# The one-hots of a node within its block of 128 go from VectorE to GpSimd in the counting stage of a four-layer graph network

## The reference, cut to what matters

```python
summed = segment_sum(x[src], dst)            # layer 0: mean over the edges of a node
cnt    = segment_sum(ones, dst)
h      = (summed / max(cnt, 1)) @ W_l + b_l + x @ W_r       # then batch norm, relu
...
out_deg = segment_sum(ones, src)             # layer 1: normalised convolution
h       = x * rsqrt(max(out_deg, 1))
agg     = segment_sum(h[src], dst) * rsqrt(max(in_deg, 1))  # then @ W + b
...
# layer 2: attention over the edges with a tensor product; layer 3: relu messages over the edges
```

## Time and profile before

| | |
|---|---|
| median of 3 runs | 6073.1 us (6062.63 to 6097.11) |
| profiled execution, own time | 6084.07 us |
| its span, first to last instruction | 6082.3 us |
| counting stage, first to last one-hot | 103.8 to 702.1 us |
| VectorE busy in 300 to 500 us | 198.05 of 200 us |
| ScalarE busy in 300 to 500 us | 150.89 of 200 us |
| GpSimd busy in 104 to 705 us | none |

### The profile page before, as it was taken

The page is one execution under the profiler, slowest core; times in us unless marked ns, Lnnn a source line. Parts: engine busy times, 40 slices in busy tenths (PEclk is TensorE's granted clock), DMA queues, the critical chain, the costliest instruction groups (busy, mean ns, idle before and its releaser), DMA issues. The chain is left out here.

```text
span 6082.3 us, 95707 instructions
## 1 busy us (share of the span) xinstructions
PE 4642.1 (76%) x21193; PEld 3132.0 (51%) x21193; DVE 4743.6 (78%) x9453; ACT 2345.0 (39%) x4962; POOL 3215.8 (53%) x4106
## 2 busy tenths in 40 slices
PE   2887567588888888888888888888885555555566
PEld 1322223366666666666666666666662554554454
DVE  6999853499999999999999999999995443433344
ACT  1777500155555555445555555455541000000001
POOL 0000000167766776667667777676662565555563
PEclk7999879599999999999999999999995555555555
DMA  2111134366666666666666666666641333333332
GB/s 60 74 74 84 63 149 165 84 146 141 144 141 142 147 143 138 139 140 143 142 144 145 141 140 140 139 146 140 138 103 38 82 80 77 79 78 79 77 82 48
DMA packets 540385, 692.83 MB, mean 114 GB/s; under 512 B 191096, under 2 KB 302648, under 8 KB 536248
## 3 DMA queue, kind: packets, MB, share of 16 engines
q1 hardware_dynamic: 485752, 608.80, 40.9%
q0 software_dynamic: 52288, 81.11, 6.0%
q10 hardware_dynamic: 2240, 1.78, 0.1%
HBM read 636.60 MB, written 54.79 MB: 114 GB/s over the span
## 5 line engine op out<-in xcount | busy, mean ns | idle before, releaser
L1539 POOL DMA_INDIRECT msg_rows<-a_rows,msg_idx x808 | 795.1, 984 | 571.3 <-ACT msg_idx L1511 295.1
L1114 POOL DMA_INDIRECT attn_rows<-x_twice,attn_idx x808 | 899.5, 1113 | 223.6 <-issue 214.4
L1063 ACT CAST attn_z_hi<-attn_z 128x512 fp32r<-128x512 f32 x1010 | 622.4, 620 | 666.0 <-DVE attn_z L1346 373.5
L1352 DVE TENSOR_TENSOR attn_z_lo<-attn_z,attn_z_hi 128x512 fp32r<-128x512 f32 x808 | 823.4, 1019 | 18.7 <-ACT attn_z_hi L1063 1.3
L1577 PE MATMUL msg_at_dst<-msg_bwin,msg_pick 128*128 128x64 f32 x1616 | 397.7, 428 | 573.6 <-DVE msg_pick L1603 337.5
L1151 POOL TENSOR_TENSOR attn_vx<-attn_ex,attn_vw 128x512 f32<-128x512 f32 x202 | 327.4, 1621 | 791.8 <-ACT attn_ex L1090 791.8
L1346 DVE TENSOR_TENSOR attn_z<-attn_xt,attn_sh 128x512 f32<-128x512 f32 x1010 | 684.1, 694 | 21.4 <-ACT attn_xt L1046 1.2
L1577 PEld LDWEIGHTS msg_at_dst<-msg_bwin,msg_pick 128*128 128x128 f32 x1616 | 360.0, 328 | 649.0 <-DVE msg_pick L1603 370.5
L843 POOL TENSOR_TENSOR x_t<-x_t,ln_rec 64x416 f32<-64x416 f32 x12 | 12.7, 1058 | 1147.7 <-DVE ln_rec L832 1147.7
L1630 DVE TENSOR_TENSOR acc<-acc,msg_sums 64x128 f32 x808 | 225.8, 279 | 463.1 <-remote 282.4
L1517 ACT ACTIVATE msg_msg<-msg_pre 128x256 f32<-128x256 f32 x202 | 84.2, 417 | 1238.3 <-DVE msg_pre L1618 679.2
(11 more groups left out here) (265 smaller groups left out, 11957.9 us busy)
## 6 DMA issues: line engine op xcount, KB each, us to landing
attn_sh<-in_edge_sh SPq DMA_DIRECT2D x404, 640.0 KB
attn_dst<-dst_scaled SPq DMA_DIRECT2D x202, 256.5 KB
attn_feat<-in_edge_feat SPq DMA_DIRECT2D x404, 128.0 KB
attn_qwin<-q_rows SPq DMA_DIRECT2D x808, 64.0 KB
msg_dst<-dst_scaled SPq DMA_DIRECT2D x202, 256.0 KB
counts<-chunk SPq DMA_DIRECT2D x15, 3100.0 KB, 9.7
chunk_late<-counts SPq DMA_DIRECT2D x15, 3100.0 KB, 10.4
msg_bwin<-b_rows SPq DMA_DIRECT2D x808, 32.0 KB
```

The source lines that it names most:

```text
L1063: nc.scalar.copy(z_hi[p][:, c, :], z[:, c % 2, :]).then_inc(high_sb, 1)
L1114: pool.indirect_dma_start(rows[p][:, t, :], None, dram["x_twice"], bass.IndirectOffsetOnAxis(ap=idx[p][:, t:t + 1], axis=0)).then_inc(rows ...
L1352: dve.tensor_tensor(z_lo[p][:, c, :], z[:, c % 2, :], z_hi[p][:, c, :].bitcast(F32), ALU.subtract).then_inc(low_ready, 1)
L1539: pool.indirect_dma_start(rows[p][:, t, :], None, dram["a_rows"], bass.IndirectOffsetOnAxis(ap=idx[p][:, t:t + 1], axis=0)).then_inc(rows_ ...
```

## The change

GpSimd gets a program of its own in the counting stage. It makes `lo_hot`, three `tensor_scalar` per group, behind the same wait for the ring as VectorE has. VectorE keeps `key_hot`, behind its own copy of that wait, and the additions. The semaphore `hot` becomes two, `key_made` and `lo_made`, and TensorE waits for both.

```diff
@@ VectorE
                 for s in range(SLOTS):
-                    nc.vector.tensor_scalar(lo_hot[g % RING][:, s, :], sb["lo_iota"][:], sb["lo_tab"][:, s, g:g + 1],
-                                            None, ALU.is_equal)
                     ts = nc.vector.tensor_scalar(key_hot[g % RING][:, s, :], sb["key_iota"][:],
                                                  sb["key_tab"][:, s, g:g + 1], None, ALU.is_equal)
-                ts.then_inc(hot, 1)
+                ts.then_inc(key_made, 1)
@@ GpSimd
+        @block.gpsimd
+        def _(pool):
+            for g in range(NG):
+                if g >= RING:
+                    pool.wait_ge(counted, g - RING + 1)
+                for s in range(SLOTS):
+                    ts = nc.gpsimd.tensor_scalar(lo_hot[g % RING][:, s, :], sb["lo_iota"][:],
+                                                 sb["lo_tab"][:, s, g:g + 1], None, ALU.is_equal)
+                ts.then_inc(lo_made, 1)
@@ TensorE
-                pe.wait_ge(hot, g + 1)
+                pe.wait_ge(key_made, g + 1)
+                pe.wait_ge(lo_made, g + 1)
```

More of the change, by code:

```diff
@@ L449, in count_and_sum @@
         ph = Phase(nc, ctx, "count")
-        piece_step, pieces_done, cleared, hot, counted, evacuated, applied, added, tallied, reduced = (
-            ph.sem(n) for n in ("piece_step", "pieces_done", "cleared", "hot", "counted", "evacuated",
+        piece_step, pieces_done, cleared, key_made, lo_made, counted, evacuated, applied, added, tallied, reduced = (
+            ph.sem(n) for n in ("piece_step", "pieces_done", "cleared", "key_made", "lo_made", "counted", "evacuated",
                                 "applied", "added", "tallied", "reduced"))
```

## The result

| | before | after |
|---|---|---|
| median | 6080.66 us (6062.63 to 6097.11, 4 runs) | 6412.02 us (6402.59 to 6426.31, 4 runs) |
| profiled execution, own time | 6084.07 us | 6426.31 us |
| first to last 128-column one-hot | 103.8 to 701.9 us, VectorE | 88.9 to 972.5 us, GpSimd |
| first to last row-wise maximum of the attention loop | 1211.4 to 4552.7 us | 1481.8 to 4871.9 us |

The change makes the kernel slower: the ratio is 1.0537, with a 95% interval of 1.0509 to 1.0565, 331 us by the medians. The forecast was 6221 us, 140 us above the median before, and its range ended at 6390 us. The sign was right, but by another mechanism than the forecast's, so it is no merit of the sum; the size was not right.

What follows compares the result with a forecast made beforehand. VectorE was taken to bound the counting stage; 0.805 us work plus 0.80 us stall made 1.605 us a group against 1.287, +148 us over 465 groups. Forecast 6221 us; whole range 6020 to 6390.

Steps and rivals of the forecast that it cites:

- the sum: Counting stage: 0.80 us stall on 0.805 us VectorE work, 1.605 us per group against 1.287, times 465: +148 us.
- What bounds the kernel: Counting stage, 598.3 us: VectorE is full and sets the pace at 1.287 us per group until another engine takes over.
- The pace of the next engine: Counting stage: with VectorE relieved, TensorE and ScalarE would set about 1.05 us per group, a gain of 109 us.
- What VectorE gives up: Counting stage: three 128-column one-hots at 0.16 us each leave VectorE, whose work falls from 1.285 to 0.805 us per group.
- What GpSimd takes on: Counting stage: a GpSimd one-hot costs 0.30 us, between 0.20 and 0.41; three make 0.90 us per group, below 1.05.
- GpSimd is itself the bound: Rival, counting stage: the GpSimd instruction costs 0.55 us, a group 1.97 us, +315 us, 6388 us; chance 0.16.
- What the two engines do to each other: Counting stage: VectorE stands still during GpSimd's burst of three one-hots, 0.80 us of stall per group; chance 0.60.
- the eight in a row: Attention loop row cited as evidence: a VectorE subtraction lasted 3.96 us instead of 0.69, waiting for eight successive GpSimd additions.
- the full stall: Counting stage: VectorE waits for all three GpSimd one-hots of a group, less about 0.10 us for the first one's start.
- The ring, the additions, the stages up to the attention loop: GpSimd runs ahead by the ring's four groups, so its waits cost nothing; additions and neighbouring stages do not change.
- Nothing after 760 us changes: Everything after the counting stage, the attention loop included, was claimed to keep its time: 0 us.
- TensorE's clock: Rival, counting stage: the granted clock falls, some 30 us more; expected to hold with TensorE 64% busy; no separate chance.

Runs made afterwards that it cites:

- e6: Changed kernel, but GpSimd makes its 128-column one-hots for the first four groups only, later groups reuse them: 6012.57 us, ratio 0.9902 to the kernel before.
- e1: Changed kernel, but GpSimd makes only one of the three 128-column one-hots per group, VectorE the other two: 5995.02 us against 6077.91 before, ratio 0.9867.
- e11: Changed kernel, but GpSimd makes one 128-column one-hot in even groups and two in odd ones, VectorE the rest: 6101.61 us, ratio 1.003 to the kernel before.
- e5: Changed kernel, but VectorE makes its 400-column one-hots for the first four groups only, later groups reuse them: 6345.23 us in one run.
- e3: Changed kernel, but GpSimd makes only the first 64 of the 128 columns of each one-hot: 6163.96 us in one run.
- e2: Changed kernel, but GpSimd makes two of the three 128-column one-hots per group, VectorE the third: 6108.78 us, ratio 1.0053 to the kernel before.
- e13: Kernel before plus 1395 one-column memsets on GpSimd in the counting stage that nothing waits for: 5860.52 us, one run, on a chip where the kernel before takes 5786.
- e15: Kernel before plus 465 one-column memsets on GpSimd in the counting stage that nothing waits for, on another chip: 5760.45 us against 5785.75, ratio 0.9954.
- e12: Kernel before plus 12 one-column memsets on GpSimd in the counting stage that nothing waits for, on another chip: 5859.12 us against 5785.68, one run.
- e8: Changed kernel, but GpSimd takes the minimum of the row and the number per partition in place of the comparison: 6388.93 us, one run.
- e4: Changed kernel, but GpSimd compares a row of fp32 numbers in place of fp16 ones: 6398.98 us, one run.
- e7: Changed kernel, but GpSimd compares with the constant 5 in place of the number per partition from the table: 6389.36 us, one run.

## Why the prediction was wrong, point by point

- **What bounds the kernel:** right. VectorE set the pace, and with its 128-column one-hots gone (e6) the stage is 146 us shorter. The pace of the next engine was mis-sized: 0.964 us, not 1.05.
- **What VectorE gives up:** right by direction; e1 and e11 came out at 1.165 and 1.170 us a group, from sums of the distances of the earlier trace rows that give 1.125 and 1.045 and some hold-up.
- **What GpSimd takes on:** this step failed, and it is the main one. I took 0.30 us with bounds of 0.20 and 0.41, from an affine select and an iota and a two-input addition. Measured: 0.585 us nearly alone (e5), 0.634 in the stage. The upper bound was no bound: a two-input row doesn't cover another instruction with one input. The case was there as the rival *GpSimd is itself the bound*, at 0.55 us and +315 us, with a chance of 0.16; it is what happened, and the stage itself gave +271. It put the instruction too cheap (0.55 for 0.585 us) and the hold-up too dear (0.315 for 0.15 us a group); that its 1.97 us is so near to the 1.90 measured is in part luck. The Trainium skill (GPSIMD Engine Reference, sections 3.1 and 4.1) puts one-input work at about line rate, 1.03 cycles per element; the 2.66 ns a column of e3 are three times that at 1.2 GHz, so the measurement decides against it for this instruction.
- **What the two engines do to each other:** this step failed too, the other way. I took the eight in a row as the rule and forecast 0.80 us of stall a group. VectorE's three one-hots take 0.94 us in place of 0.79, 0.15 more. GpSimd pays 0.05 us per instruction. The two failed steps work against each other: with 0.585 us a piece and the full stall the sum of the forecast would have been 3 × 0.585 − 0.10 + 0.805 = 2.46 us a group, +545 us. That a `tensor_scalar` with one input is among those held up was right: e2 and e13 show it. The Trainium skill (SBUF — State Buffer, section Who interferes with whom) says so as well, for the two-port modes. By it the later one is blocked for the whole instruction of the other; here VectorE loses 0.04 us (e1) to 0.12 us (e2) to a GpSimd instruction of 0.59 us, and the measurement decides. Its exception for GpSimd instructions that only write is for VectorE instructions with two inputs, and the memsets of e13 agree that it doesn't extend to these.
- **The ring, the additions, the stages up to the attention loop:** right, 270.4 us later at the loop's start against 271 at the stage's end.
- **Nothing after 760 us changes:** wrong. 49 us of the result are the attention loop, a term that I had put at nothing, and they belong to the number of instructions on GpSimd, not to the work moved.
- **TensorE's clock:** granted 0.90 in 300 to 500 us against 0.97; in 104 to 160 us it was 0.50, the lower level, with TensorE busy 64% of the stretch, where I had expected it to hold. It cost nothing, for GpSimd was the bound (busy 53.08 of those 56 us).

## What to carry to other kernels

Price an instruction by a row of the same instruction on the same engine; where the trace has none, another instruction's row is no upper bound, and the rival in which the new engine is the bound deserves the weight. When an idle engine is given work, give it only what fits its measured pace: one of three one-hots makes this kernel 1.3% faster than before (58 us in the stage, 31 us in the attention loop by the count of instructions), all three make it 5.4% slower. Compare stages, not only totals, before a difference of half a per cent is put down to an edit: here an edit of idle instructions alone moved the total by −0.5% (e15) or, in one run, +1.3% (e12).

## What the runs showed of the hardware that was not expected

- A GpSimd `tensor_scalar` of 128x128 with bf16 output costs 0.585 us from start to start (e5), and 0.58 to 0.60 us in the first twelve whether it compares or takes a minimum (e8), with fp16 or fp32 input (e4), with a number per partition or a constant (e7). From 128 and 64 columns (e3) that is 0.24 us + 2.66 ns per column.
- A dense run of VectorE holds GpSimd out too. At the start of the stage VectorE made 24 one-hots in a row, and the next GpSimd instruction, which began among them at 106.92 us, took 3.41 us. Timeline of the changed kernel:

```profile
104.78 6.01 DVE L475 TENSOR_SCALAR count_key_hot<-key_iota,key_tab 128x400 bf16<-128x400 f16 x24
...
106.92 5.17 POOL L500 TENSOR_SCALAR count_lo_hot<-lo_iota,lo_tab 128x128 bf16<-128x128 f16 x4 [10.97 <-PE count_bank L527]
```

- The length of a loop on VectorE and GpSimd, 3310 to 3417 us, goes with the number of GpSimd instructions ahead of it in the program. The cause isn't known.
- GpSimd memsets of one column, 33 ns apart, hold VectorE's `tensor_scalar` up too: one of 400 columns lasts up to 1.03 us beside them, where 0.33 us is the longest without (e13).
